# Another order of TensorE's instructions over four steps of a software-pipelined attention, and of SyncE's stores

## The reference, cut to what matters

```python
q = _lin(_lin(x, wq_w, wq_b), vq_w, vq_b)      # k and v likewise; x is (4, 1024, 512)
q = q.reshape(b, s, hc, H).transpose(2, 0, 1, 3)   # hc = 32 heads, H = 16
scores = jnp.einsum('cbqh,cbkh->cbqk', q, k) / scale
attn = jax.nn.softmax(scores, axis=-1)
o = jnp.einsum('cbqk,cbkh->cbqh', attn, v)
```

## Time and profile before

| | us |
|---|---|
| median of three runs | 2127.49 |
| lowest and highest run | 2122.95, 2129.62 |
| span of the profiled execution | 2122.5 |
| TensorE busy in the span | 2067.2 |
| VectorE | 1659.3 |
| ScalarE | 1314.4 |
| attention, first score to last product | 343.0 to 1691.6 |

### The profile page before, as it was taken

How to read it: one execution, slowest core, us unless ns; L and a number is a source line. 1 busy time by engine, 2 the same in 40 slices (tenths; PEclk the granted TensorE clock), 3 DMA queues, 4 the chain that set the end, 5 groups by cost and what they waited for, 6 DMA issues and landing times.

```text
span 2122.5 us, 39702 instructions
## 1 busy us (share of the span) xinstructions
PE 2067.2 (97%) x11249; PEld 1165.3 (55%) x11264; DVE 1659.3 (78%) x1727; ACT 1314.4 (62%) x2429; POOL 491.5 (23%) x878
## 2 busy tenths in 40 slices
PE   9999999999999999999999999999999999988996
PEld 4788775444444444444444444444444387767874
DVE  4333356888899999999999998999898576886687
ACT  0112113778888888888888888888888742454344
POOL 0000001121212221221122122212121371465245
PEclk9999998999999999999999999999999999999997
DMA  4456735555575665664665646655647578773672
GB/s 164 139 159 155 186 112 109 84 123 137 100 139 120 108 136 97 131 143 95 135 128 101 141 103 123 137 99 126 138 99 179 182 267 306 278 254 124 222 262 101
DMA packets 214414, 315.25 MB, mean 149 GB/s; under 512 B 105424, under 2 KB 121808, under 8 KB 202064
## 3 DMA queue, kind: packets, MB, share of 16 engines
q1 hardware_dynamic: 214352, 314.47, 58.9%
HBM read 211.06 MB, written 101.19 MB: 147 GB/s over the span
## 4 chain that ended last, share of the span: by engine, by line
PE 86%; DVE 6%; ACT 2%; SPq 2%; DMA 2%; issue 1%; POOL 1%; DVEq 0%; POOLq 0%; ACTq 0%
PE psum L542 26%; PE psum L551 23%; PE psum L187 22%; PE psum L223 11%; PE psum L88 2%; DVE stats L1392 1%; ACT probs L616 1%; DVE y L1517 1%; PE psum L1312 1%; DVE gates L1491 1%; DVE gates L1488 1%; SPq L208 1%; ACT gates L1241 1%; DVE y L1422 0%; DMA x_block<-in_x_t_dram 0%
## 5 line engine op out<-in xcount | busy, mean ns | idle before, releaser
L230 DVE TENSOR_REDUCE neg_max<-psum 128x1 f32<-128x1024 f32 x1024 | 1206.0, 1220 | 135.2 <-PE psum L223 135.0
L616 ACT ACTIVATE probs<-psum 128x512 f32<-128x512 f32 x2048 | 1065.3, 606 | 273.5 <-PE psum L542 269.3
L542 PE MATMUL psum<-q_op,k_op 50*128 50x512 f32 x2048 | 750.3, 449 | 3.9 <-ACT probs L616 1.4
L542 PEld LDWEIGHTS psum<-q_op,k_op 50*128 50x128 f32 x2048 | 353.6, 191 | 580.2 <-ACT probs L616 565.3
L223 PE MATMUL psum<-k_op,q_op 48*128 48x512 f32 x2048 | 620.2, 479 | 1.0 <-DVE neg_max L230 1.0
L551 PE MATMUL psum<-probs,v_op 128*32 128x512 f32 x4096 | 548.1, 607 | 5.8 <-ACT probs L616 2.9
L223 PEld LDWEIGHTS psum<-k_op,q_op 48*128 48x128 f32 x2048 | 389.0, 315 | 21.1 <-issue 4.4
L187 PE MATMUL psum<-x_wino,conv_w 128*128 128x512 f32 x1152 | 276.0, 395 | 1.0 <-DMA conv_w<-conv_w_parts_dram 1.0
L187 PEld LDWEIGHTS psum<-x_wino,conv_w 128*128 128x128 f32 x1152 | 214.4, 188 | 47.0 <-issue 1.3
L241 POOL CAST neg_max_parts<-neg_max 128x8 fp32r<-128x8 f32 x128 | 24.5, 191 | 887.8 <-DVE neg_max L230 887.8
L551 PEld LDWEIGHTS psum<-probs,v_op 128*32 128x32 f32 x4096 | 82.5, 108 | 136.8 <-ACT probs L616 70.0
(11 more groups left out here) (103 smaller groups left out, 1629.8 us busy)
## 6 DMA issues: line engine op xcount, KB each, us to landing
q_op<-qk_parts_dram SPq DMA_DIRECT2D x384, 128.0 KB, 4.1
conv_w<-conv_w_parts_dram SPq DMA_DIRECT2D x32, 1536.0 KB, 6.9
qk_parts_dram<-qk_parts SPq DMA_DIRECT2D x128, 256.0 KB, 3.2
k_op<-qk_parts_dram SPq DMA_DIRECT2D x384, 64.0 KB, 4.0
conv_w_parts_dram<-conv_w_parts SPq DMA_DIRECT2D x16, 1536.0 KB, 6.1
attended_dram<-out SPq DMA_DIRECT2D x64, 256.0 KB, 2.2
attended_parts_dram<-o_parts SPq DMA_DIRECT2D x128, 128.0 KB, 2.5
gates<-in_ctx_dram SPq DMA_DIRECT2D x32, 512.0 KB, 7.7
```

The costliest lines, as they stand in the source:

```text
L230: nc.vector.tensor_reduce(ops["max"][b][:, t:t + 1], mem["pair"][t % 2][:], AX_X, ALU.max, negate=True).then_inc(ops["maxed"], 1)
L542: nc.tensor.matmul(score_bank(i, n, j, last), kop[i][r, j // 2, n // 2 * P:(n // 2 + 1) * P], qop[i][r, j // 2, j % 2 * HALF:(j % 2 + 1) * ...
L616: nc.scalar.activation(probs[n % DEEP][:, j, :], score_bank(k, n, j, last), ACT.Exp, scale=SCALE).then_inc(exp_done, 1)
```

## The change

TensorE's order is written out over four steps. The scores are counted through a slot by `t`; in odd steps their four parts are taken in another order (`c ^ n % 2`), so that a score's lane is the parity of `t`. Products stand behind scores 5, 8, 11 and 14 of sixteen, and are those of the steps n-2, n-1, n and n+1 when the four steps begin with n. Units stand at other places, and each is told in which lane it starts. The copy of bank 7 goes behind the ninth exponential. SyncE stores the second maxima ahead of `load_pair` and `load_recips`. At the end two products stand instead of one. The numbers of instructions of each kind do not change.

```diff
--- before.py
+++ after.py
@@ -404,6 +404,7 @@
     RING = 3
     DEEP = 4
     WIDE_FROM = 2 * STEPS + 5
+    EVACUATE_AFTER = 8
     with ExitStack() as ctx:
         sb = lambda name, shape, dt: ctx.enter_context(nc.sbuf_tensor(name, shape, dt))
         for i in range(2, 4):
@@ -443,12 +444,13 @@
             sp.dma_start(taps[:], conv_w[bass.ds(w, 1), :, :, :].rearrange("a p (t c) n -> p (a t) (c n)", t=2))\
                 .then_inc(taps_in, DMA)
 
-        def score_bank(k, n, j, last):
-
-            wide = (k * STEPS + n - WIDE_FROM) * TILES + j
+        def score_bank(k, t, last):
+
+            cell = k * (STEPS * TILES) + t
+            wide = cell - WIDE_FROM * TILES
             if last and wide >= 0:
                 return wide_bank[wide % (2 * RING)]
-            return s2_bank[(k * (STEPS * TILES) + n * TILES + j) % RING]
+            return s2_bank[cell % RING]
 
         @block.sync
         def _(sp):
@@ -480,13 +482,13 @@
                     sp.wait_ge(pv_out, s + 1)
                     sp.sem_inc(waited, 1)
                     store_out(sp, norm, us_scr, s - 1, (k - 1) % 2)
+                if not (last and k == 3):
+                    sp.wait_ge(split, s * 2 + 4)
+                    store_max(sp, ops, (k + 1) % 4, 1)
                 if k % 2 == 0 and not (first and k == 0):
                     load_pair(sp, norm, us_scr, it * 2 + (k - 2) // 2)
                 if k % 2 == 1 and not (first and k == 1):
                     load_recips(sp, norm, r_scr, it * 2 + (k - 3) // 2)
-                if not (last and k == 3):
-                    sp.wait_ge(split, s * 2 + 4)
-                    store_max(sp, ops, (k + 1) % 4, 1)
                 if last and k < 2:
                     sp.wait_ge(norm["parts_stored"], PAIRS // 2 * PART_STORES + DMA)
                     for half in range(2):
@@ -528,23 +530,44 @@
             pe.wait_ge(qk_lo, 8 + PROJECTED // 3 * 2)
             pe.wait_ge(v_out, 4 + PROJECTED // 3)
 
-            def s2(i, n, j, last, ready):
-                lane = (n + j) % 2
-                r = slice(LANE * lane, LANE * lane + ROWS_SHIFT)
-                wide = (i * STEPS + n - WIDE_FROM) * TILES + j
+            def shifted(it, k, t, last):
+
+                n, c = t // TILES, t % TILES
+                j = c ^ n % 2
+                r = slice(LANE * (t % 2), LANE * (t % 2) + ROWS_SHIFT)
+                cell = k * (STEPS * TILES) + t
+                wide = cell - WIDE_FROM * TILES
+                if n == 0 and c % 2 == 0:
+                    pe.wait_ge(max_in[k][j // 2], (it + 1) * MAXES + DMA)
 
                 if last and RING <= wide < 2 * RING:
                     pe.wait_ge(maxed, SLOTS * 2 * QT)
                 elif last and wide >= 2 * RING:
-                    pe.wait_ge(exp_done, ready - RING)
+                    pe.wait_ge(exp_done, it * 4 * (STEPS * TILES) + cell + 1 - RING)
                 else:
-                    pe.wait_ge(exp_done, ready)
-                nc.tensor.matmul(score_bank(i, n, j, last), kop[i][r, j // 2, n // 2 * P:(n // 2 + 1) * P],
-                                 qop[i][r, j // 2, j % 2 * HALF:(j % 2 + 1) * HALF],
+                    pe.wait_ge(exp_done, it * 4 * (STEPS * TILES) + cell + (2 if cell < 2 else 1))
+                nc.tensor.matmul(score_bank(k, t, last), kop[k][r, j // 2, n // 2 * P:(n // 2 + 1) * P],
+                                 qop[k][r, j // 2, j % 2 * HALF:(j % 2 + 1) * HALF],
                                  start=True, stop=True).then_inc(s2_full, 1)
 
-            def pv(s, k, n):
-
+            def unit(it, k, u, lane, last):
+
+                s = it * 4 + k
+                ahead = k + 1 if u < QT else k + 2
+                if last and ahead >= 4:
+                    return
+                if u == QT:
+                    pe.wait_ge(op_in[ahead % 4], (it + ahead // 4 + 1) * OPS)
+                pe.wait_ge(maxed, s * 16 + u + LEAD - 1)
+                b, t = 1 - u // QT, u % QT
+                score_lane(nc, mem, ops, ahead % 4, b, t, lane)
+                score_lane(nc, mem, ops, ahead % 4, b, t, 1 - lane).then_inc(s1_full, 1)
+
+            def values(s, k, n):
+
+                if n == 0:
+                    pe.wait_ge(v_ready, s + 1)
+                    pe.wait_ge(pv_out, s + 1)
                 pe.wait_ge(exp_done, s * (STEPS * TILES) + n * TILES + TILES + RING)
                 for j in range(TILES):
                     kt = n // 2 + QT // 2 * ((n + j) % 2)
@@ -554,33 +577,44 @@
 
             def slot(it, k, first=False, last=False):
                 s = it * 4 + k
-                for n in range(STEPS):
-                    for half in range(2):
-                        unit = 2 * n + half
-                        ahead = k + 1 if unit < QT else k + 2
-                        for side in range(2):
-                            j = 2 * half + side
-                            cell = k * (STEPS * TILES) + n * TILES + j
-                            ready = s * (STEPS * TILES) + n * TILES + j + (2 if cell < 2 else 1)
-                            if side == 1 and not (last and ahead >= 4):
-                                if unit == QT:
-                                    pe.wait_ge(op_in[ahead % 4], (it + ahead // 4 + 1) * OPS)
-
-                                pe.wait_ge(maxed, s * 16 + unit + LEAD - 1)
-                                b, t = 1 - unit // QT, unit % QT
-                                score_lane(nc, mem, ops, ahead % 4, b, t, (n + 1) % 2)
-                                score_lane(nc, mem, ops, ahead % 4, b, t, n % 2).then_inc(s1_full, 1)
-                            if n == 0 and j % 2 == 0:
-                                pe.wait_ge(max_in[k][j // 2], (it + 1) * MAXES + DMA)
-                            s2(k, n, j, last, ready)
-                    if n == 1:
-                        pe.wait_ge(v_ready, s + 1)
-
-                        pe.wait_ge(pv_out, s + 1)
-                    if n > 0:
-                        pv(s, k, n - 1)
+
+                def values_at(n):
+
+                    if n >= 0:
+                        values(s, k, n)
                     elif not (first and k == 0):
-                        pv(s - 1, (k - 1) % 4, STEPS - 1)
+                        values(s - 1, (k - 1) % 4, STEPS + n)
+
+                for n in range(0, STEPS, 4):
+                    t, u = n * TILES, 2 * n
+                    shifted(it, k, t, last)
+                    shifted(it, k, t + 1, last)
+                    unit(it, k, u, 0, last)
+                    shifted(it, k, t + 2, last)
+                    shifted(it, k, t + 3, last)
+                    shifted(it, k, t + 4, last)
+                    unit(it, k, u + 1, 1, last)
+                    shifted(it, k, t + 5, last)
+                    values_at(n - 2)
+                    shifted(it, k, t + 6, last)
+                    unit(it, k, u + 2, 1, last)
+                    shifted(it, k, t + 7, last)
+                    shifted(it, k, t + 8, last)
+                    unit(it, k, u + 3, 1, last)
+                    values_at(n - 1)
+                    shifted(it, k, t + 9, last)
+                    shifted(it, k, t + 10, last)
+                    shifted(it, k, t + 11, last)
+                    unit(it, k, u + 4, 0, last)
+                    values_at(n)
+                    shifted(it, k, t + 12, last)
+                    unit(it, k, u + 5, 1, last)
+                    shifted(it, k, t + 13, last)
+                    shifted(it, k, t + 14, last)
+                    unit(it, k, u + 6, 1, last)
+                    values_at(n + 1)
+                    shifted(it, k, t + 15, last)
+                    unit(it, k, u + 7, 0, last)
 
             for k in range(4):
                 slot(0, k, first=True)
@@ -589,7 +623,8 @@
                     slot(it, k)
             for k in range(4):
                 slot(LAST, k, last=True)
-            pv(LAST * 4 + 3, 3, STEPS - 1)
+            for n in range(STEPS - 2, STEPS):
+                values(LAST * 4 + 3, 3, n)
 
         @block.scalar
         def _(act):
@@ -611,11 +646,12 @@
                     for n in range(STEPS):
 
                         act.wait_ge(pv_step, s * STEPS + n + 1)
-                        for j in range(TILES):
-                            act.wait_ge(s2_full, s * (STEPS * TILES) + n * TILES + j + 1)
-                            nc.scalar.activation(probs[n % DEEP][:, j, :], score_bank(k, n, j, last), ACT.Exp,
+                        for c in range(TILES):
+                            t = n * TILES + c
+                            act.wait_ge(s2_full, s * (STEPS * TILES) + t + 1)
+                            nc.scalar.activation(probs[n % DEEP][:, c ^ n % 2, :], score_bank(k, t, last), ACT.Exp,
                                                  scale=SCALE).then_inc(exp_done, 1)
-                            if n == 1 and j == 0 and not (first and k == 0):
+                            if t == EVACUATE_AFTER and not (first and k == 0):
```

## The result

The changed kernel takes 2111.61 us (median of seven runs, 2109.48 to 2115.93), the one before, run beside it, 2124.94. The ratio is 0.9938 with a 95% interval of 0.9921 to 0.9955, some 13 us less, where 30 were forecast. A second series gave 2110.59 against 2125.49, ratio 0.9944 (0.9926 to 0.9961).

What follows compares the result with a forecast made beforehand. The bound was taken to be a loop of waits, no engine's own work. TensorE's new order (26 us) and the copy (4 us) sum to 30 us, off 2127.5, giving 2097.5 us; range 2078 to 2122.

Steps and rivals of the forecast that it cites:

- Bound and loop: Steady attention: TensorE and ScalarE wait for each other, 2.61 us a step, 10.45 a round of four steps.
- Lane pace and product: TensorE: a lane ends a matmul every 0.24 us; a product starts 0.07 before the preceding end, next score 0.99 after it.
- The copy: Copy of bank 7 behind the ninth exponential falls into ScalarE's pause during a product; saves 0.06 us a slot, 4 us.
- stretch 4: From a round's fourth product to the next round's first: seven scores and three units, paced by ScalarE, 4.08 us.
- stretch 2: From a round's second product to its third: scores 9, 10, 11 and one unit, 1.90 us.
- The spare 0.06 of stretch 4: Score 2, behind a unit waiting for VectorE's reduction, still ends before its exponential is due, with 0.06 us to spare.
- no change: Rival: reductions 1.22 us apart instead of 1.14 use up the spare and the gain; 2124 to 2130 us; chance 0.09.
- slower: Rival: reductions over 1.22 us apart make waiting units hold scores; at 1.30 the kernel takes 2152 us; chance 0.08.
- VectorE become the bound: Rival: TensorE is faster than forecast, leaving VectorE's 9.1 us a round as limit; saving over 45 us; chance 0.07.
- Weights that load only after a lane's stream: Rival: each further matmul in a lane costs 0.24 plus 0.18 to 0.31 us; kernel at 2400 us; chance 0.02.
- stretches 1 and 3: From a round's first product to its second, and third to fourth: three scores and two units, 2.13 us each.
- the zero: SyncE's second-maxima stores, moved ahead of two loads, land in time for the next slot's third score: price 0.

Runs made afterwards that it cites:

- fill2: Changed kernel with two zero-weight matmuls added behind the second score of each round, where TensorE waits for VectorE; 2111.15 us, ratio 0.9939 to the kernel before.
- fill_busy: Changed kernel with four added matmuls a slot, placed in its second round where TensorE does not wait; 2163.12 us, ratio 1.0179 to the kernel before.
- evac7: Changed kernel with the copy of bank 7 behind the eighth exponential instead of the ninth; 2179.16 us, ratio 1.0261 to the kernel before.
- order_only: Changed kernel with SyncE's two parts swapped back, keeping TensorE's new order and the copy's new place; 2168.96 us, ratio 1.0251 to the kernel before.
- fill4: Changed kernel with four zero-weight matmuls a round, two behind the second score, one each behind third and fourth; 2100.32 us, ratio 0.9909 to the kernel before.

## Why the prediction was wrong

**Bound and loop.** Right. The old loop of 10.45 us a round was the thing to break, and its parts were the right prices.

**Lane pace and product.** Right: 0.24, 0.07 and 0.99 us carried over to an order in which they had never been run. The medians over the loop are 2.14, 1.90, 2.14 and 4.08, a round of 10.26 against 10.24 forecast and 10.45 before. 112 rounds x 0.19 = 21 us, where the same step gives 24.

**The copy.** The term of 4 us was mis-sized: it is 0. The stretch with the copy takes 1.99 instead of 1.90, 0.09 a slot where it was 0.08 before.

```profile
579.98 1.06 PE L574 MATMUL psum<-probs,v_op 128*32 128x512 f32 x8
...
581.20 0.58 ACT L641 COPY out<-psum 128x512 f32<-128x512 f32 x1 [0.26 <-PE psum L574]
...
581.68 1.58 ACT L652 ACTIVATE probs<-psum 128x512 f32<-128x512 f32 x3
```

The pause is there, and the product takes the 1.06 of the forecast. But the copy starts 0.16 after the product's end (581.04 and 581.20), where I had counted 0.04. So ScalarE is free for the tenth exponential at 1.70 from the product's start, not at 1.57, and it was due at 1.54.

**A term I left out:** the end of the loop's turn. The last place of a turn takes 20.94, the others 20.47, 20.64 and 20.59; its stretch 4 across the slot's end takes 4.29 instead of 4.08. In the trace TensorE's branch stands there between unit 7 and score 0, and the weights of score 0 load 0.50 after those of score 15 (848.49 and 847.99) instead of 0.22 (868.96 and 868.74). Before, the branch came behind a product that was still running. 14 x 0.21 = 3 us. 21 - 3 = 18 us, which is the table's 1175.3 - 1157.0.

**The step that failed** is the sum, which priced every stretch at the full clock. I had read PEclk for the kernel before, found it full in the steady part, and took it for given in the kernel after. The change gathered the waiting more than it added to it. Before, each 2.61 us hold one wait of 0.28 at L542. Now 6.2 us of a round run without a gap between the matmuls, and stretch 4 holds the wait for VectorE (0.51) and those for ScalarE behind it (0.21 and 0.31).

In the five profiled executions with TensorE's and SyncE's new orders that had more than one fall between 400 and 1600 us (the changed kernel twice, `fill2`, `fill_busy`, `evac7`), 29 of 30 falls begin within 0.36 us of the start of the product that ends stretch 4, the other 0.41 ahead of it. (With SyncE's old order, in `order_only`, and in slot 62, where the units end, they begin up to 1.2 us from it.) The falls cost this execution 9.4 us of the 56 slots and about 1.5 in the last four (slot 60 takes 22.27, in the second series without a fall 20.75), 11 us in all.

The whole account: of the forecast's 30 us, 26.9 lie in the 56 slots of the loop. 26.9 - 2.2 (rounds) - 3.4 (copy) - 3.0 (branch) - 9.4 (clock) + 2.1 (SyncE's stores in time) = 11.0, as in the table. Outside the loop, the first four slots took 88.9 instead of 91.3 (the clock was low in both kernels, but not for equally long), the last four with their fall 0.2 more than before, and the part ahead of the attention, which the change does not touch, 1.5 less. That is 14.7 of the spans' difference of 14.8. The measured 2111.61 lies within the range of 2078 to 2122, but by luck: none of the bounds that it was built from is the clock or the branch.

Shown is that filling the waits removes the falls, that the same work elsewhere does not, and that a little more waiting in stretch 4 of the odd slots brought eleven falls for five or six, ten of them there. That it is the gathering, and not the sum of the waits, has this for it, in the 56 slots and outside of falls, with the time a slot in which no matmul is recorded:

| kernel | without a matmul, us a slot | falls (400 to 1660) | us at the lower level in them |
|---|---|---|---|
| before | 0.06 | 0 | 0 |
| changed | 0.25 | 5 and 6 | 24 and 27 |
| two added (`fill2`) | 0.08 | 6 | 38 |
| four added (`fill4`) | 0.09 | 1 | 3 |
| copy one exponential earlier (`evac7`) | 1.04 | 6 | 41 |
| SyncE's old order (`order_only`) | 0.38 | 11 | 123 |

The sum does not order the falls. `evac7` waits four times as long as the changed kernel, but in stretch 2, and has six; `order_only` adds 0.13 us a slot (0.29, if all 16.0 us of waits for the stores are counted) where `evac7` adds 0.79, but in stretch 4, and has eleven. What in stretch 4 it is, and why `fill2` did not help, stays open: no run changed the gathering alone.

**VectorE.** The spare 0.06 of stretch 4 held: 4.08. The rivals "no change" and "slower" by slower reductions did not occur, nor did VectorE become the bound. Its idle time did not fall by the fifth that I had named as a sign (117.2 against 117.7).

**Weights that load only after a lane's stream.** Excluded: stretches 1 and 3 took 2.14 with loads of 0.18 and 0.31 under way in both lanes. The trace disagrees with the rule of the Trainium skill ("TensorE: Matmul & The Clock Gate", "The mechanism") in this form of use, as it did before. The same section also lets the weights go ahead into a background buffer; these rows may be that case, which no run here can tell.

**SyncE.** Right that the moved store covers the zero: from 448 us on no score of the changed kernel waits for a store. The price without it was wrong in its parts: up to 2 us in each even slot's stores was forecast, the wait costs 0.3 to 0.4, and the 57 us of the experiment are mostly the clock again.

The Trainium skill, same page, section "HAM oscillation — how this bites in real kernels", describes a clock that falls when TensorE idles for long between bursts of work, for DMAs. Here it fell in a kernel whose TensorE is 97% busy and, in an undisturbed round, waits at most 0.51 us at a time in one place; the trace agrees in kind and shows it for much shorter waits.

## What to carry to other kernels

When an order is rewritten so that dense stretches and one waiting stretch take turns, work out not only the length of the round but where TensorE will stand still, and compare PEclk slot by slot: a few falls can eat nearly half of a gain of one per cent. A wait that cannot be removed can be filled with harmless matmuls, in it and not beside it; here four a round worked and two did not. When a run is slower, take its falls out before pricing a wait by it: medians over slots are no guard once half of them are disturbed. And here the prices of TensorE's stretches, measured where it waited for nothing, carried over to a new order to a hundredth of a microsecond; the wait ahead of the copy was 0.12 more than counted, and the branch was not counted at all.

## What was not expected of the hardware

- In the changed kernel the clock fell for 3.4 us in most cases and for 10.2 in others, in the loop each time within a few tenths of the same place in the round, and 198 to 219 us after the fall before, once 273 and once, into slot 62, 137. With SyncE's old order single falls lasted up to 37.6 us.
- A fall of 3.4 us costs 1.5 to 1.6 us in a slot (22.17 and 22.19 against 20.6), one of 10.2 us 4.6 (25.1 against 20.5), somewhat less than half of it, probably since waits for the other engines absorb a part. In the other runs it is 0.42 to 0.48 of the time at the lower level.
- Four matmuls more in each round, some 500 in all, cost 3 to 4 us of the loop where TensorE waits, nearly all of it at the end of the loop's turn; where it does not wait, a pair costs 0.24 or 0.47 us.
